# Attention block: VectorE's negated row maxima move in front of the next group's first maximum

## The reference

```python
x = layernorm(x + attention(x))
x = layernorm(x + soft_moe(x))
```

```python
att = softmax(where(causal, q_for_k @ k_lat.T * 32 ** -0.5, -inf))
y   = (att @ v_lat) @ l2o_w.T + l2o_b
```

## Time and profile before

| | us |
|---|---|
| median of three runs | 1183.93 |
| profiled execution, its own time | 1186.27 |
| its span, first to last instruction | 1184.6 |
| PE busy in the span | 1138.6 (96%) |
| DVE busy | 780.8 (66%) |
| ACT busy | 670.7 (57%) |
| POOL busy | 571.1 (48%) |

### The profile page before, as it was taken

One profiled execution on the slowest core, in us unless ns is written; L12 is line 12 of the kernel. 1 busy time (PEld: TensorE's weight loads), 2 busy tenths in 40 slices (PEclk: granted clock), 3 DMA queues, 4 the chain that ended last, 5 costly groups with the idle time before them and its releaser, 6 DMA issues.

```text
span 1184.6 us, 19139 instructions
## 1 busy us (share of the span) xinstructions
PE 1138.6 (96%) x6882; PEld 903.8 (76%) x6882; DVE 780.8 (66%) x1257; ACT 670.7 (57%) x948; POOL 571.1 (48%) x395
## 2 busy tenths in 40 slices
PE   8799999999999999988899999989999999999996
PEld 5566767676767767656788888878888888888885
DVE  6878787969697978755677777785545454523334
ACT  2556466566656565646787777766555555530112
POOL 5556555655656555512666666645444444430000
PEclk9899999999999999989899999999999999999999
DMA  4645444645565464630044335358555545365761
GB/s 144 153 102 136 118 121 107 161 112 156 124 161 127 119 167 94 178 90 34 25 159 159 124 124 187 107 179 276 158 168 186 163 143 166 108 218 177 243 219 54
DMA packets 127198, 170.23 MB, mean 144 GB/s; under 512 B 47313, under 2 KB 77970, under 8 KB 127122
## 3 DMA queue, kind: packets, MB, share of 16 engines
q1 hardware_dynamic: 124546, 167.88, 48.6%
q10 hardware_dynamic: 2576, 1.35, 0.5%
HBM read 72.13 MB, written 37.75 MB: 93 GB/s over the span
## 4 chain that ended last, share of the span: by engine, by line
PE 81%; DVE 9%; ACT 5%; issue 1%; ACTq 1%; POOL 1%; SPq 1%; DMA 1%; DVEq 0%; POOLq 0%
PE ring L463 12%; PE ring L465 11%; PE ring L464 11%; PE ring L1684 7%; PE tail L1539 6%; PE ring L1528 5%; PE ring L1512 4%; PE tail L463 4%; PE tail L464 4%; PE tail L465 4%; ACT pt L898 3%; PE ring L1561 2%; PE tail L1684 2%; PE tail L1499 2%; PE ring L1615 1%; DVE mx L1206 1%
## 5 line engine op out<-in xcount | busy, mean ns | idle before, releaser
L1206 DVE TENSOR_REDUCE mx<-ring 128x4 f32<-128x512 f32 (+2 forms) x192 | 199.8, 1043 | 74.0 <-PE ring L1515 73.5
L898 ACT ACTIVATE pt<-ring 128x1024 f32<-128x1024 f32 (+1 forms) x192 | 169.0, 881 | 92.3 <-PE ring L1528 88.4
L743 POOL TENSOR_SCALAR_AFFINE_SELECT pt<-pt 128x512 f32<-128x512 f32 x128 | 81.3, 636 | 188.7 <-ACT pt L898 188.7
L1528 PE MATMUL ring<-qks 98*128 98x256 f32 (+3 forms) x512 | 137.0, 371 | 3.5 <-DVE mx L1206 2.0
L1512 PE MATMUL ring<-qks 96*128 96x384 f32 (+3 forms) x512 | 120.5, 338 | 5.5 <-DMA qks<-stg 4.6
L786 POOL TENSOR_TENSOR hl<-hid,hh 128x512 fp32r<-128x512 f32 x64 | 82.6, 1302 | 77.6 <-ACT hh L1015 77.6
L760 POOL TENSOR_TENSOR dl<-e,dh 128x1024 fp32r<-128x1024 f32 x28 | 67.2, 2410 | 84.9 <-ACT e L969 84.9
L1528 PEld LDWEIGHTS ring<-qks 98*128 98x128 f32 x512 | 79.6, 192 | 32.1 <-issue 20.4
L1340 DVE SCALAR_TENSOR_TENSOR hid<-ring,bias_e,gate 128x512 f32<-128x512 f32 x64 | 47.9, 748 | 75.5 <-ACT gate L1009 43.9
L1512 PEld LDWEIGHTS ring<-qks 96*128 96x128 f32 x512 | 80.8, 193 | 21.2 <-issue 6.4
L729 POOL TENSOR_TENSOR rope<-rope,rot 128x1024 f32<-128x1024 f32 x31 | 75.1, 2422 | 36.5 <-DVE rope L1196 36.5
(11 more groups left out here) (254 smaller groups left out, 3098.0 us busy)
## 6 DMA issues: line engine op xcount, KB each, us to landing
qks<-stg SPq DMA_DIRECT2D x378, 128.0 KB, 2.5
c_dram<-c2s SPq DMA_DIRECT2D x32, 512.0 KB, 5.0
c<-c_dram SPq DMA_DIRECT2D x32, 512.0 KB, 6.1
sl_dram<-sls SPq DMA_DIRECT2D x32, 256.0 KB, 3.4
wg<-in_wg SPq DMA_DIRECT2D x16, 512.0 KB, 5.6
wu<-in_wu SPq DMA_DIRECT2D x16, 512.0 KB, 6.5
wd<-in_wd SPq DMA_DIRECT2D x16, 512.0 KB, 7.2
eo<-est SPq DMA_DIRECT2D x32, 256.0 KB, 3.8
```

Of the source, the lines that this page charges most:

```text
L743: nc.gpsimd.affine_select(out=m, in_=m, compare_op=ALU.is_ge, fill=0.0, base=0, pattern=[[0, GH], [1, P]], channel_multiplier=-1).then_inc ...
L898: nc.scalar.activation(pt[j][:, h:h + heads, 0:n], heads_of(tile, heads, n), ACT.Exp, scale=SCALE).then_inc(empty, 1)
L1206: nc.vector.tensor_reduce(out=mx[:, g, h:h + heads, i], in_=heads_of(tile, heads, (i + 1) * P), axis=AX.X, op=ALU.max).then_inc(empty, 1)
L1528: last = nc.tensor.matmul(scores[:, h, :], qks[0:KS_ROWS + 2, g, 1, h0 + h, j * P:(j + 1) * P], qks[0:KS_ROWS + 2, g, 0, h0 + h, j * P:T], ...
```

## The change

`negmax` gets the offset 4.6 in place of 6.05 in DVE's table. In the sorted order it then stands directly behind the last maximum of its own group: in front of the next group's first maximum, and, except at the first boundary and the last one, in front of a later group's `qlo`. All other steps keep their order, on DVE and on the other engines; no instruction and no wait is added or removed. The last group's `negmax` stays where it was.

```diff
-DVE_AT = {..., "max": -3.11, "negmax": 6.05, "v": 11.5, ...}
+DVE_AT = {..., "max": -3.11, "negmax": 4.6, "v": 11.5, ...}
```

More of the change, by code:

```diff
@@ L43 @@
 ACT_AT = {"stack": -9.0, "xth": -30.5, "lat": -22.0, "khi": -12.85, "qhi": -9.58, "neg": 9.57, "exp": 11.74, "y": 22.25, "yTT": 52.85, "apply": 76.25, "wlat": -30.402, "senorm": -2.024, "seT": 7, "seh": 9.429}
-DVE_AT = {"xtl": -32.0, "blat": -28.9, "kvrows": -28.8, "slotg": -28.781, "shuffle": -21.3, "cos": -17.25, "qlo": -10.0, "max": -3.11, "negmax": 6.05, "v": 11.5, "yT": 26.15, "cproj": 55.1, "ln": 56.75, "wlat": -30.314, "wv": -17.071, "sestat": -23.24, "sescale": -7.5, "sel": 9.985}
+DVE_AT = {"xtl": -32.0, "blat": -28.9, "kvrows": -28.8, "slotg": -28.781, "shuffle": -21.3, "cos": -17.25, "qlo": -10.0, "max": -3.11, "negmax": 4.6, "v": 11.5, "yT": 26.15, "cproj": 55.1, "ln": 56.75, "wlat": -30.314, "wv": -17.071, "sestat": -23.24, "sescale": -7.5, "sel": 9.985}
 POOL_AT = {"sin": -26.06, "add": -23.69, "klo": -21.92, "mask": 2.69, "bias": 42.5}
```

## The result

The changed kernel takes 1266.66 us (median of 6 runs, 1261.54 to 1268.85), the kernel before 1183.73 on the same chip (6 runs, 1183.34 to 1184.98). The ratio is 1.0688, 95% interval 1.0668 to 1.0708: slower by 82.9 us. The forecast was 1254, the range 1225 to 1274.

The account below looks back on a forecast made before the run. The prediction took PE to bound the attention half, busy 61.26 of 62.00 us a batch. Stalls of 48.4 us plus 22 us of slower clock made 70 us, so 1254 us from 1183.93; range 1225 to 1274.

Parts of the forecast that it names:

- Step 1: At negmax on DVE: both instructions stand behind POOL's sine product and mask, ending at 356.86 and 357.44, no earlier than before.
- Steps 2 and 4: Late first maximum makes PE stand 2.08 us before exp unit 4 (net 1.75), 1.96 us before cproj.
- step 5: Count of stalls: 27 group boundaries, 21 at 1.75 us and 6 with cproj at 1.96 us; sum 48.4 us.
- Step 3: PE's wait at the transpose of negmax goes, giving back 0.33 us a boundary; nothing new waits there.
- The late stacks: Stacks of q and k rows issued about 2.1 us later eat 0.3 us of margin a boundary; at most 8 us.
- Step 6: PE's clock falls to 1.2 GHz behind four in five stalls, 1.0 us each: 22 us, at most 38.
- Rival (a): The stalls come but PE's clock stays: 1183.9 + 48.4 = 1232 us; chance 0.22.
- Rival (b): Negmax is not held, PE's 0.33 us at the transpose is saved at some 23 boundaries: 1177 us; chance 0.07.
- Rival (c): DVE and POOL take turns at half speed rather than one standing: 1181 to 1184 us; chance 0.06.

Follow-up runs that it names:

- e10: The changed kernel with POOL's product with the sines left out but for 16 of its 1024 columns: 1175.49 us, ratio 0.9929.
- e5: The changed kernel with POOL's sine product cut into four instructions of a quarter each: 1189.53 us, ratio 1.0051.
- e8: The changed kernel with the first negmax instruction reading one SBUF tensor (mx times -1) in place of two: 1265.45 us, ratio 1.0713.
- e3: The changed kernel with PE filling the second maximum's slot three times over at the 27 stall boundaries, same numbers: 1228.82 us, ratio 1.0381.
- e9: The kernel before with POOL's product with the sines left out but for 16 of its 1024 columns: 1180.82 us, ratio 0.9974.
- e7: The kernel before, negmax in its old place, with POOL's mask made to wait until negmax is through: 1177.30 us, ratio 0.9957.
- e6: The changed kernel with POOL's sine product made to wait for negmax by a semaphore: 1192.15 us, ratio 1.0071.
- e1: The changed kernel with POOL's sine product moved behind the mask that follows it: 1192.24 us, ratio 1.0075.

## Why the prediction was right, and where its size was off

- Step 1 was right: L1214 1.952 us in the median, ending with L723, L1216 0.550, ending with the mask. Its reason held for the place (e10) and the end of the hold (e5), not for the operands: one tensor in SBUF is held as well (e8), and a shuffle within SBUF is not (L1180).
- Steps 2 and 4: PE's idle time is 1.73 us at exp unit 4 and 1.71 at `cproj`, put to DVE's maximum, in the 21 and 6 places that step 5 counted. Exp unit 4 comes 1.97 us late, against the 2.08 worked out: it follows the end of the first maximum by 0.05 us (413.24 to 413.29), not by the 0.15 taken, which makes 2.7 us over 27 places.
- Step 3 was right: PE's wait ahead of the transpose fell from 22 times with 3.8 us to one with 0.4. Together steps 2 to 5 gave 48.4 us; e3, which has the late maximum and not the slow clock, measured 45 to 46.
- The late stacks, taken as nothing, were nothing that the waits show: PE waits for stacked rows twice in the run, 3.2 us in all, where it waited 4.6 us before.
- Step 6 had the mechanism and not the size: 22 us were taken, e3 gives 38, which is the upper bound that the step had worked out (a fall behind each of the 27 stalls at 1.4 us). Both factors were too small. The clock fell behind 25 of the 27 stalls, not four in five. And the 1.0 us came from score units in the earlier trace rows; behind these stalls stand the products with v, 16 matmuls that take 2.91 us in place of 1.71, 1.2 us by themselves. The 12.7 us between forecast and result are these 16, less 2 or 3 of the standing. The result lies in the range because its top counted all of the 38 us. That e3 gives the very figure of that bound is chance: it is 25 falls at some 1.5 us, not 27 at 1.4.
- Rival (a), 1232, fell: the clock went to 0.50 behind idle gaps of 1.68 to 1.73 us, and e3 shows 1229 as the time when the gaps are filled. By the rule of the Trainium skill (TensorE: Matmul & The Clock Gate, "HAM oscillation — how this bites in real kernels"), which warns only of longer gaps, the time would have been that of rival (a); the measurement decides against it.
- Rival (b), 7 us faster if negmax is not held, is what e10 did against e9: 5.3 us. Its price was near, its condition did not hold. Rival (c), turns, fell: the first instruction stands to the end.

## What to carry to other kernels

Before moving a small VectorE instruction that works within SBUF, look in the trace for the same operation beside GpSimd: whether it is held depends on more than where its tensors lie. If it is held, the length to reckon with is what is left of the GpSimd instruction in progress, and what queues behind it on VectorE pays. Price a stall of TensorE with the granted clock behind it, and by the instructions that stand there, not by those of the row that showed the clock. Where two engines hold each other, a wait that delays the side with time to spare can be the cheaper cure (e7), but find out first whom it pushes into whom (e6).

## What the runs showed that was not expected

A VectorE instruction with one tensor, from SBUF to SBUF, 16 numbers a partition, stood 1.93 us in the median beside a GpSimd product (e8). The hold works both ways: GpSimd's mask took 1.62 us in place of 0.63 beside VectorE's cos product (e1). A shuffle within SBUF stood beside no GpSimd instruction (L1180). And behind 25 of 27 idle gaps of 1.7 us TensorE went from 2.4 to 1.2 GHz; with the gap cut to 0.3 us by repeated work the whole half stood at 0.99, as in the kernel before.
